# Two attention and mixture-of-experts layers on one core: the second layer's expert sum moved from VectorE to ScalarE and GpSimd, with a new order of the work

## What is computed

```python
x = x + xattn0(layernorm(x), ctx, bias, mask)        # 16 heads of 8, 77 keys, additive bias 4x16x512x77
x = x + moe0(layernorm(x), w_router, wi, wo)         # 8 experts, 2 chosen, 64 slots each, 128 -> 512 -> gelu -> 128
x = x + xattn1(layernorm(x), ctx, attn_mask, pad)    # 16 heads of 8, 77 keys, additive mask 512x77
x = x + moe1(layernorm(x), gate_w, expert_w)         # below
```

```python
probs = softmax(x @ gate_w.T + gate_b)               # 10 gates, 8 of them real experts
weights, selected = top_k(probs, 2)                  # null experts dropped, the rest normalised
combine_w = ...                                      # token x 8, zero where not chosen
expert_out = einsum('td,edh->teh', x, expert_w) + expert_b
out = einsum('te,teh->th', combine_w, expert_out)
```

## Time and profile before

| what | value |
|---|---|
| time, median of 3 runs | 374.14 us (373.89 to 374.92) |
| the profiled execution | 372.75 us |
| its span in the trace | 371.0 us |
| VectorE / GpSimd / ScalarE busy | 261.1 / 183.1 / 173.2 us |
| TensorE matmul busy | 318.2 us |

### The profile page before, as it was taken

The page is one execution under the profiler, slowest core; times in us unless marked ns, Lnnn a source line. Parts: engine busy times, 40 slices in busy tenths (PEclk is TensorE's granted clock), DMA queues, the critical chain, the costliest instruction groups (busy, mean ns, idle before and its releaser), DMA issues.

```text
span 371.0 us, 8972 instructions
## 1 busy us (share of the span) xinstructions
PE 318.2 (86%) x3628; PEld 237.4 (64%) x3633; DVE 261.1 (70%) x639; ACT 173.2 (47%) x321; POOL 183.1 (49%) x197
## 2 busy tenths in 40 slices
PE   3789767899999999999999999999787987798771
PEld 2468465577888778778788778885444653556420
DVE  4669665977596396852679566667779689986762
ACT  3144313375844827349285464735341363346331
POOL 7356283785708357163364714155362266624515
PEclk9999977999999999999999999999976699689995
DMA  7994970050504000000000000000000000000000
GB/s 191 256 374 107 333 213 2 2 145 3 138 10 113 27 2 2 3 2 2 2 3 2 2 2 2 3 0 2 3 0 31 0 3 0 30 2 3 0 28 28
DMA packets 26427, 19.15 MB, mean 52 GB/s; under 512 B 1973, under 2 KB 24339, under 8 KB 26387
## 3 DMA queue, kind: packets, MB, share of 16 engines
q1 hardware_dynamic: 26387, 18.59, 17.3%
HBM read 17.53 MB, written 1.05 MB: 50 GB/s over the span
## 4 chain that ended last, share of the span: by engine, by line
PE 50%; DVE 25%; issue 10%; ACT 7%; POOL 6%; DMA 1%; POOLq 0%; DVEq 0%; ACTq 0%
PE PB L1046 9%; DVE SC L1640 6%; PE HBK L1135 6%; PE SP L1027 5%; PE SP L1008 4%; PE EBK L1150 4%; POOL SC L408 4%; DVE mx L1642 3%; ACT PT L632 3%; DVE acc L1847 3%; DVE rc L1647 3%; PE HBK L1210 2%; PE SP L1012 2%; PE HBK L1158 2%; PE EBK L1210 2%
## 5 line engine op out<-in xcount | busy, mean ns | idle before, releaser
L408 POOL TENSOR_TENSOR SC<-SC,mx 128x1232 f32<-128x1232 f32 x32 | 74.0, 2313 | 98.9 <-DVE mx L1642 98.8
L632 ACT COPY PT<-SP 128x512 f32<-128x512 f32 (+1 forms) x96 | 44.5, 526 | 44.5 <-PE SP L1027 38.4
L624 ACT ACTIVATE SC<-SC 128x1232 f32<-128x1232 f32 x32 | 39.4, 1234 | 26.8 <-POOL SC L408 26.7
L1027 PE MATMUL SP<-ident,SC 128*128 128x128 f32 x320 | 47.2, 292 | 4.6 <-ACT SC L624 4.0
L1642 DVE TENSOR_REDUCE mx<-SC 128x16 f32<-128x1232 f32 x32 | 46.0, 1436 | 1.1
L1027 PEld LDWEIGHTS SP<-ident,SC 128*128 128x128 f32 x320 | 39.1, 151 | 10.8 <-ACT SC L624 6.2
L1647 DVE RECIPROCAL rc<-PB 128x128 f32<-128x128 f32 x32 | 30.5, 954 | 21.0 <-PE PB L1046 20.7
L1135 PE MATMUL HBK<-ein,wi_s 128*128 128x128 f32 x256 | 36.1, 284 | 2.1 <-ACT hT L653 2.1
L1135 PEld LDWEIGHTS HBK<-ein,wi_s 128*128 128x128 f32 x256 | 31.1, 191 | 7.5 <-ACT hT L653 4.9
L1008 PE MATMUL SP<-KB,qT 32*128 32x308 f32 x256 | 28.8, 512 | 8.1 <-DVE SC L1640 4.3
L1046 PE MATMUL PB<-PT,VB 128*32 128x128 f32 x768 | 30.1, 294 | 5.7 <-ACT PT L632 4.9
(11 more groups left out here) (188 smaller groups left out, 569.7 us busy)
## 6 DMA issues: line engine op xcount, KB each, us to landing
BI<-in_fside_Bx16xSxS SPq DMA_DIRECT2D x8, 1232.0 KB, 6.6
wi_s<-in_L_ffn_wi SPq DMA_DIRECT2D x1, 2048.0 KB, 8.9
X<-in_x SPq DMA_DIRECT2D x4, 256.0 KB, 4.3
out<-acc SPq DMA_DIRECT2D x3, 256.0 KB, 2.2
MI<-in_mask_BxSxS_ik SPq DMA_DIRECT2D x8, 77.0 KB, 5.0
ew_s<-in_L_ffn_expert_w SPq DMA_DIRECT2D x1, 512.0 KB, 4.1
out<-acc SPq DMA_DIRECT2D x2, 128.0 KB, 1.7
ctxn<-in_ctx SPq DMA_DIRECT2D x1, 154.0 KB
```

The lines of the kernel that those rows point to most:

```text
L408: g.tensor_tensor(S4, S4, m4, ALU.subtract).then_inc(s["shifted"], 1)
L624: sc.activation(S3, S3, ACT.Exp).then_inc(s["probs"], 1)
L632: sc.copy(PT[:, c0:c1, :].rearrange("p c t -> p (c t)"), SP[:, n, 0:(c1 - c0) * P]).then_inc(s["PTs"], 1)
L1027: last = te.transpose(SP[:, n, (c - c0) * P:(c - c0 + 1) * P], SC[i % 2][:, c * P:(c + 1) * P], ident[:])
```

## The change

In the batches f = 4, 5 and 6, `scale_experts` on ScalarE scales all eight experts of a tile: first the four of HBK into `weighed[0]`, then the four of EBK into `weighed[1]`. So both buffers belong to one tile, and its first half waits until GpSimd's first addition of the tile before is done. `sum_experts` on GpSimd gets one more addition ahead of its three (128 x 512, `weighed[0] + weighed[1]` into `fours`, in hT[1]), and its last one waits for `start_acc` through `n_acc`. The 48 `weigh_expert` calls of these batches go. `n_used` is now counted by ScalarE. The last batch is as before, apart from the semaphore counts.

All four lists of calls are in a new order, in both layers. The amount of other work is the same. The core of the diff, with the places of the lists that the text below speaks of:

```diff
+            def pair_count(n):
+                return 3 * n - max(0, n - NT * (B - 1))
             def sum_experts(f, i):
                 n = NT * (f - B) + i
                 pool.wait_ge(s["n_scaled"], n + 1)
+                pool.wait_ge(s["n_used" if f < 2 * B - 1 else "n_scaled"], n + 1)
                 if n > 0:
                     pool.wait_ge(s["n_done"], n)
...
+                if f < 2 * B - 1:
+                    g.tensor_tensor(fours, weighed[0].rearrange("p k e d -> p (k e d)"),
+                                    weighed[1].rearrange("p k e d -> p (k e d)"), ALU.add).then_inc(s["n_pair"], 1)
+                    pool.wait_ge(s["n_pair"], done + 1)
+                    done += 1
+                    g.tensor_tensor(pairs, fours[:, 0:2 * D].rearrange("p (e d) -> p e d", e=2),
+                                    fours[:, 2 * D:4 * D].rearrange("p (e d) -> p e d", e=2), ALU.add)\
+                        .then_inc(s["n_pair"], 1)
...
+                pool.wait_ge(s["n_acc"], f - B + 1)
                 g.tensor_tensor(acc[:, i, :], acc[:, i, :], pairs[:, 0, :], ALU.add).then_inc(s["n_done"], 1)
@@ GpSimd's list @@
-            shift(5, 3)
             sum_experts(4, 0)
-            block_keys(3, 1, "k_kb1")
+            sum_experts(4, 1)
             f_rstd(5)
-            sum_experts(4, 1)
             sum_experts(4, 2)
             residual_bias(6, 1)
             shift(6, 0)
+            shift(6, 1)
             sum_experts(4, 3)
-            shift(6, 1)
...
             sum_experts(5, 0)
+            sum_experts(5, 1)
             f_rstd(6)
-            sum_experts(5, 1)
@@ ScalarE @@
+                if f < 2 * B - 1:
+                    act.wait_ge(s["n_eo"], 2 * n + 1)
+                    if n >= 1:
+                        act.wait_ge(s["n_pair"], 3 * (n - 1) + 1)
+                    for k in range(2):
+                        if k == 1:
+                            act.wait_ge(s["n_eo"], 2 * n + 2)
+                        for e in range(NE // 2):
+                            ins = sc.activation(weighed[k][:, e // 2, e % 2, :], expert_banks(f, i)[k][:, e * D:(e + 1) * D],
+                                                ACT.Identity, scale=cw[:, i, 4 * k + e:4 * k + e + 1])
+                        ins.then_inc(s[("n_used", "n_scaled")[k]], 1)
+                    return
@@ TensorE's list @@
             turn(6, 1, 1)
+            attn_scores(6, 3, 1)
             weigh_values(6, 1)
-            attn_scores(6, 3, 1)
             experts(5, 0)
...
             attn_scores(7, 3, 1)
+            experts(6, 0)
             weigh_values(7, 1)
-            experts(6, 0)
@@ VectorE's list @@
             softmax_max(7, 3, 1)
             invert(7, 1)
             normalise(7, 1)
-            weigh_expert(6, 0, 0)
             add_residual(7, 1, 1)
-            weigh_expert(6, 0, 1)
-            weigh_expert(6, 0, 2)
-            weigh_expert(6, 0, 3)
```

488 lines of the change are left out of this document (226 added, 262 removed).

## The result

| | before | after |
|---|---|---|
| median of 4 runs | 374.16 us (373.89 to 374.92) | 385.3 us (382.78 to 386.57) |
| ratio to before | | 1.030, 95% interval 1.0251 to 1.035 |
| the profiled execution | 372.75 us | 384.72 us |
| its span | 371.0 us | 383.0 us |

The change makes the kernel 3% slower. The forecast was 372.2 us (368.6 to 376.3): wrong in sign, and the result is 9 us outside its range.

A forecast was written before the change was run, and what follows sets the result against it. No engine was taken as full: TensorE bound the first layer, VectorE the second layer's routing stretches. Terms -2.6 - 0.5 - 2.0 + 2.0 + 0.9 + 0.3 = -1.9 us took 374.14 to 372.2 us, range 368.6 to 376.3.

The forecast's parts named there:

- The first layer's order: First layer, 60 to 212 us: new order taken as 0, bounds -2.3 to +2.3 us from TensorE's idle time.
- The tail: After 357 us: keeps its work, so nothing was counted.
- Contention: Routing chains: GpSimd's twelve new additions stretch VectorE's small operations, 0.9 us loss, bounds 0 and 6.6.
- the slower rival: GpSimd's queue decides: ScalarE's 1.17 us more delays sums and `f_rstd` in three batches; 375.7 us; chance 0.25.
- `f_rstd` behind two trees: GpSimd, three batches: two whole sums ahead of `f_rstd` make it late by 0.6, 0.3 and 1.0; 2.0 us loss.
- -2.6: VectorE's removed weighings in two routing chains and the attention around 300 us: 2.6 us direct gain, bounds 0 and 6.3.
- -0.5: GpSimd: `shift(6, 1)` no longer behind `sum_experts(4, 3)`, an addition leaves the path; 0.5 us gain, bounds 0 and 5.5.
- -2.0: TensorE's `attn_scores(6, 3)` moved earlier lets softmax work fill VectorE's 3.14 us wait at 292.50; 2.0 us gain, bounds 0 and 3.1.
- The clock: Rival, second layer: TensorE's clock stays up, 3.1 us less on the chain; 369.1 us, chance 0.13.
- the wrong ones: Signs against it: routing chain stretched over 1 us a batch, `f_rstd` over 1.3 us late, first layer shifted over 1 us.
- The batch steps: Sign of being right: steps from `start_acc` to `start_acc` shorter by 1 us or so.

The follow-up runs named there:

- half_first: Kernel before with the change's new order in the first layer only up to batch 2's logits, old order behind: 376.55 us, ratio 1.0106.
- half_second: Kernel before with the change's new order only from batch 2's logits to the end of the first layer: 376.57 us, ratio 1.0096.
- six_old: Changed kernel with the first layer's order of before and batch 6 summed as before, new sum in batches 4 and 5 alone: 375.68 us, ratio 0.9985.
- tiny_add: Changed kernel with the first layer's order of before, GpSimd's new first addition cut to 4 of 512 columns: 379.56 us, ratio 1.013.
- move_rstd: Changed functions with all call lists in the order of before, and f_rstd(7) ahead of sum_experts(6, 1) on GpSimd: 385.46 us, ratio 1.0299.
- old_early: Changed kernel with the first layer's order of before, second layer as changed: 377.34 us, ratio 1.0066.
- move_only: Changed functions with all four call lists in the order of before, the 48 weigh_expert calls left out: 384.13 us, ratio 1.0251.
- fewer_loads: Kernel before with ScalarE's softmax_exp(2,0) moved behind gelu(0,5), 17 table loads instead of 19: 377.07 us, ratio 1.012.
- more_loads: Kernel before with two ScalarE calls moved in the first layer, 23 table loads instead of 19: 373.11 us, ratio 0.9957.
- six_loads: six_old with ScalarE's order of more_loads: 376.91 us, ratio 1.0065 to the kernel before.

## Why the prediction was wrong

**The first layer's order, taken as 0 with bounds of 2.3 us: +6.5.** This step failed first. The bound was made from TensorE's idle time, 7.04 us. Idle time bounds what a better order can gain; it says nothing of what a worse one can lose. TensorE was busy 144.96 of 152 us there, so hardly any delay of what feeds it is covered, and the right reading of that row was one-sided: no gain over a few us, a loss open above. `half_first` and `half_second` show that the loss is spread over the layer.

**The tail, taken as 0: +4.0.** The prediction said that the tail keeps its work. It does after the routing, but the last tiles of batch 6 are summed beside `f_norm(7)` and the last routing chain. `f_norm(7)` came later and in pieces, and TensorE then worked some 10 us mostly at its lower level, with little behind it to take in the delay. `six_old` shows that the move in batch 6 does it, 26.6 for 30.0, and `tiny_add` that GpSimd's first addition has 2.2 us of it.

**Contention, 0.9 us with bounds to 6.6: mis-sized.** The estimate looked only at the small operations of the routing chain. These did stretch: after 250 us those that took over 0.24 us, where 0.20 is normal, lost 5.9 us in all, against 2.7 in the kernel before; the worst are of lines 1770 and 1740, 1.20, 0.62, 1.94 and 1.28 us. The other hit is `f_norm`: 1.95, 1.96 and 1.81 us in the batches 5 to 7 before, 3.22, 2.07 and 2.98 after, 1.11 undisturbed. That is 2.6 us more, so some 5.8 in all by the rows where 0.9 was counted. Not all of it decides the time, as line 1740 in T shows. The Trainium skill (SBUF - State Buffer, Who interferes with whom) names `tensor_scalar` among VectorE's operations that can take the port pair that GpSimd uses, when their operands allow it, and says that the one that comes second is then blocked for the other's whole instruction. The prediction weighed this section for operations with two inputs alone and passed over that line; the trace agrees with it. In T the last three pieces of `f_norm(7)` let TensorE start at 357.04, 357.84 and 358.37, just behind the ends of GpSimd's instructions at 356.89, 357.69 and 358.24, and line 1740 ends at 362.79, just behind the addition's end at 362.74. The prediction also says that a milder form of the rule is counted in the slower rival; that rival's sum, 372.2 + 3.5, holds no term for it.

**`f_rstd` behind two trees, +2.0: right in size.** Its second instruction started 0.76 us after `f_mv` each time before and 1.45, 1.45 and 1.16 after: 1.8 us. Still, the rival built on it wasn't the cause. `f_rstd` was never over 1.3 us late, and in `move_rstd`, where it is early, T is longer by another wait.

**The gains, -2.6, -0.5 and -2.0: not to be seen.** M is 93.9 us in `old_early` and 95.9 after, 94.5 before; a gain of a few us could hide in M's scatter, but none is shown. The wait of 3.14 us ahead of `invert(6, 1)` at 292.50 is gone, as foretold, but it did not bring the 2.0 us. In the changed kernel VectorE waits nearly as long one call earlier, for the scores themselves:

```profile
299.61 1.44 DVE L1672 TENSOR_TENSOR SC<-SP,amp 128x1232 f32<-128x1232 f32 x1 [2.72 <-PE SP L1040]
...
302.44 0.95 DVE L1679 RECIPROCAL rc<-PB 128x128 f32<-128x128 f32 x1
```

From `start_acc(5)` (288.69 and 296.01) to the end of both calls' work it takes 8.0 us before and 7.7 after: the term was worth 0.3 us. The step that failed in it is that the scores would be there to fill the gap; `attn_scores(6, 3)` started on TensorE only at 298.06. VectorE's waits for `weigh_values` from 250 us on are 11.1 us in sum after (8 of them) and 7.5 before (6), the largest at 264, 268, 345 and 350, where the weighings used to stand. So part of what was removed had been filler in waits for TensorE. That the new late order itself is worth something is likely: `move_only`, with the old one, has M at 98.2.

**The clock.** It went against the change, not for it: 0.84 against 0.86 in M and 0.72 against 0.82 in T. The prediction had it only as a rival that gains; by the account of T above, it is over half of the tail's loss.

Of the signs that the prediction named, the wrong ones came: a first layer over 1 us later by order alone (6.5), and a routing chain stretched, from `exp_sum` to `weights` 9.28 us for 7.24 in batch 5, while the batches 6 and 7 stayed within 0.1 us, the 1.94 us of line 1770 in batch 6 included. The batch steps became longer, not shorter: from one `start_acc` to the next 38.9, 40.9 and 35.4 us for 38.2, 39.4 and 32.2.

## What to carry to other kernels

The idle time of a nearly full engine bounds what a new order can gain, never what it can lose; where the order of a stage that is 95% busy changes, take the loss as open and look for a run of the order alone. Moving work off the fullest engine pays only where that work is on the chain; here many of the removed additions filled waits, while the added ones ran beside VectorE's normalisation and stretched it (`tiny_add`), at the end, where little covers a delay. A wait of TensorE can cost more than its length, since the clock behind it can fall: 2.4 us of wait came to 5.0 in `fewer_loads`. And a stall that stands out in a trace, or a count that fits the loss (four table loads, 5.1 us of 6.5), is a theory to be tried: `more_loads` ruled the count out, and the stall did not go away when its call was moved.

## What was not expected of the hardware

**The scatter of this kernel goes with TensorE's clock.** `six_old` and `six_loads` have the same second layer. From `start_acc(5)` on VectorE does the same work, but the scores and the projection come at different times. `six_old`, then `six_loads`:

```profile
292.01 1.44 DVE L1673 TENSOR_TENSOR SC<-SP,amp 128x1232 f32<-128x1232 f32 x1 [1.15 <-PE SP L1041]
...
296.69 0.29 DVE L1692 TENSOR_TENSOR X<-PB,xr 128x128 f32<-128x128 f32 x1 [0.58 <-PE PB L1085]
```

```profile
292.74 1.44 DVE L1673 TENSOR_TENSOR SC<-SP,amp 128x1232 f32<-128x1232 f32 x1 [2.03 <-PE SP L1041]
...
299.08 0.29 DVE L1692 TENSOR_TENSOR X<-PB,xr 128x128 f32<-128x128 f32 x1 [2.24 <-PE PB L1085]
```

The clock of the 10 us from there on was 1.00 in the one and 0.68 in the other:

```profile
290.30:300.30 10.00, 9.23 (x129) 1.00 0.01 2
```

```profile
289.80:299.80 10.00, 9.48 (x80) 0.68 0.01 2
```

That is 2.5 us in 9 from `start_acc(5)` (289.98 and 289.83) to the last row, and M is longer by 2.9 in all. Both executions came out of a stretch in which TensorE had waited and its clock had read 0.50: from 275 to 285 us it was busy 4.9 us in the one and 5.0 in the other. In the next 5 us the clock read 0.80 and 0.84, and then 1.00 in `six_old` and 0.50 in `six_loads` until 296. So with the same lists in this stage and nearly the same work done, the clock came out differently, and M goes from 90.9 to 94.8 us over single executions of kernels with one second layer while T doesn't. The executions of one kernel show it too: of the ten of `six_old` the shortest, 372.78 us, has a mean clock of 0.936, and the longest, 381.94, one of 0.908. A comparison of two orders in such a stage needs several kernels or many runs.

**One misplaced call costs microseconds.** `fewer_loads` moves a single ScalarE call behind three others, saves that engine 2.6 us of table loads, and makes A 5.0 us longer, 3.4 of them as slower matmuls.
